# Batch attention: one maximum over 16 batch elements from a single four-bank PSUM buffer, in place of one over 8 from two alternating buffers

## The reference, cut to what matters

```python
scores = jnp.einsum('bqhd,bkhd->hbqk', Q, K)
attn = jax.nn.softmax(scores, axis=1)        # axis 1 is the batch, 32 elements
heads = jnp.einsum('hbqk,bkhd->bqhd', attn, V).reshape(B, S, dm)
```

## Time and profile before

| | us |
|---|---|
| median of 3 runs | 1695.55 |
| lowest and highest run | 1689.3, 1696.78 |
| the profiled execution, its own time | 1693.03 |
| its span in the profile | 1691.3 |
| busy: TensorE matmul, VectorE, GpSimd, ScalarE | 1392.7, 1242.4, 1029.3, 885.9 |

### The profile page before, as it was taken

One profiled execution on the slowest core, in us unless ns is written; L12 is line 12 of the kernel. 1 busy time (PEld: TensorE's weight loads), 2 busy tenths in 40 slices (PEclk: granted clock), 3 DMA queues, 4 the chain that ended last, 5 costly groups with the idle time before them and its releaser, 6 DMA issues. The chain is left out here.

```text
span 1691.3 us, 42035 instructions
## 1 busy us (share of the span) xinstructions
PE 1392.7 (82%) x14758; PEld 1078.4 (64%) x14759; DVE 1242.4 (73%) x2603; ACT 885.9 (52%) x1437; POOL 1029.3 (61%) x746
## 2 busy tenths in 40 slices
PE   7858999999999999998189968888888099999940
PEld 5635666666666666665179966667667099999940
DVE  5559999999999999998356646999998523333346
ACT  7818888888888888887034422222222044444420
POOL 6624888888888888889534432656556544444420
PEclk9859999999999999999589988999999599999975
DMA  6863333333333333310533321222221122222248
GB/s 221 270 197 95 77 83 82 83 82 84 82 82 83 84 80 86 81 50 18 138 123 99 94 60 59 90 94 82 89 93 54 50 63 68 66 65 65 65 138 289
DMA packets 117937, 163.58 MB, mean 97 GB/s; under 512 B 18592, under 2 KB 85408, under 8 KB 113184
## 3 DMA queue, kind: packets, MB, share of 16 engines
q1 hardware_dynamic: 92960, 123.42, 26.3%
q0 software_dynamic: 13600, 28.45, 5.1%
q10 hardware_dynamic: 11232, 9.73, 1.8%
HBM read 99.52 MB, written 62.01 MB: 96 GB/s over the span
## 5 line engine op out<-in xcount | busy, mean ns | idle before, releaser
L921 ACT ACTIVATE Ex<-pB 128x512 f32<-128x512 f32 x512 | 514.3, 1081 | 84.5 <-PE pB L731 80.2
L962 POOL TENSOR_TENSOR V<-Ex,R 128x4096 f32<-128x4096 f32 x64 | 474.2, 7409 | 98.8 <-DVE R L841 98.7
L819 DVE TENSOR_REDUCE mg<-pA 128x128 f32<-128x1024 f32 x256 | 297.5, 1203 | 3.7 <-PE pA L714 3.4
L835 DVE TENSOR_REDUCE Z<-Ex 128x64 f32<-128x2048 f32 x128 | 290.7, 2273 | 4.6 <-ACT Ex L921 4.5
L731 PEld LDWEIGHTS pB<-qk 72*128 72x128 bf16 x2048 | 157.7, 97 | 122.5 <-issue 1.1
L726 PE MATMUL pB<-mh,identb 128*128 128x512 bf16 x512 | 196.6, 384 | 36.0 <-ACT Ex L921 35.4
L1113 POOL DMA_INDIRECT y_d<-x1yb,x1xb x136 | 130.2, 957 | 151.4 <-DVE x1yb L1228 146.8
L731 PE MATMUL pB<-qk 72*128 72x128 bf16 x2048 | 198.9, 219 | 0.0
L726 PE MATMUL pB<-ml,identb 128*128 128x512 bf16 x512 | 194.0, 379 | 0.0
L741 PE MATMUL pO<-V,Vh 128*8 128x128 f32 x4096 | 161.0, 278 | 12.9 <-POOL V L962 12.8
L714 PE MATMUL pA<-qk 72*128 72x128 bf16 x2048 | 162.5, 224 | 8.8 <-DVE mg L819 4.9
(11 more groups left out here) (232 smaller groups left out, 2368.1 us busy)
## 6 DMA issues: line engine op xcount, KB each, us to landing
qk<-qs_d SPq DMA_DIRECT2D x96, 192.0 KB
qk<-ks_d SPq DMA_DIRECT2D x96, 192.0 KB
x1xb<-xs_d SPq DMA_DIRECT2D x136, 64.5 KB
f_ye<-y_d SPq DMA_DIRECT2D x16, 512.0 KB, 5.9
qs_d<-parts SPq DMA_DIRECT2D x16, 384.0 KB, 2.9
ks_d<-parts SPq DMA_DIRECT2D x16, 384.0 KB, 3.2
x0xb<-xs_d SPq DMA_DIRECT2D x72, 64.5 KB
xn_d<-xn SPq DMA_DIRECT2D x16, 258.0 KB, 3.3
```

Source lines behind the costliest of these rows:

```text
L819: dve.tensor_reduce(mg[:, :, g], pA[:, g % 2, :, :].rearrange("p b q -> p q b"), AX.X, ALU.max).then_inc(b_red, 1)
L835: dve.tensor_reduce(Z[:, q], Ex[:, j, q, :], AX.X, ALU.add).then_inc(b_sum, 1)
L921: act.activation(Ex[:, j, :, BG * g:BG * (g + 1)].rearrange("p q b -> p b q"), pB[:, g % 2, :, :], ACT.Exp).then_inc(b_exp, 1)
L962: pool.tensor_tensor(En[:, j % 2, :, :].rearrange("p b q -> p q b"), Ex[:, j, :, :], R[:, j % 2, :].unsqueeze(2).broadcast_to([P, P, B]), ...
```

## The change

A group now has 16 batch elements, and there are two groups to a unit. `pA` has the same four banks, but they are one buffer: every group of first scores waits for the maximum of the group before it. In the loop turn of a unit the first scores stand at `g = 0` and `g = 4` in blocks of 16 matmuls, where blocks of eight stood at 0, 2, 4 and 6. VectorE has one maximum ahead of the first half sum and one behind it, where it had one and three. `mg` shrinks to two columns.

```diff
-            GM = 2 * BG
+            GM = 4 * BG
...
-            pA = pb("pA", [P, 2, GM, P], ph)
+            pA = pb("pA", [P, GM, P], ph)
...
-                    if not isinstance(n, int) or n >= 2:
-                        pe.wait_ge(b_red, n - 1)
+                    if not isinstance(n, int) or n >= 1:
+                        pe.wait_ge(b_red, n)
                     for c in range(GM):
                         tok = (GM * g + c) * P
-                        ins = nc.tensor.matmul(pA[:, g % 2, c, :],
+                        ins = nc.tensor.matmul(pA[:, c, :],
...
                         for g in range(0, NBG, 2):
-                            s1(g // 2)
+                            if g % (NBG // NM) == 0:
+                                s1(g // (NBG // NM))
...
-                    dve.tensor_reduce(mg[:, :, g], pA[:, g % 2, :, :].rearrange("p b q -> p q b"),
+                    dve.tensor_reduce(mg[:, :, g], pA[:].rearrange("p b q -> p q b"),
                                       AX.X, ALU.max).then_inc(b_red, 1)
...
                             group_max(u + 2, 1)
-                            group_max(u + 2, 2)
-                            group_max(u + 2, 3)
                             unit_max(u + 2, (j + 2) % 4)
```

## The result

The changed kernel's median is 1679.94 us over 8 runs (1678.02 to 1685.04). The kernel before, run beside it, has 1689.1 us over 8 runs. The ratio is 0.9943, with a 95% interval of 0.9924 to 0.9961: 9.6 us less, or 0.6%. The three runs from which the forecast had its base (1695.55) are among those eight, and two of them are the highest (1696.78 and 1695.55). So the forecast time of 1680.5 was met more closely than the step was: 15 us were forecast and about 10 came.

What follows compares the result with a forecast made beforehand. VectorE was taken to bound the kernel at 10.56 us a unit, then TensorE and ScalarE's loop at 10.24. With -15.0 the span goes from 1691.3 to 1676.3, execution 1678, plus 2.5 gives 1680.5 us; range 1670 to 1694.

Steps and rivals of the forecast that it cites:

- What bounded the kernel before: Batch-attention stage: VectorE never waits and sets the period of 10.56 us; TensorE's loop behind it takes 9.7.
- VectorE's side: VectorE's work per unit: long maximum 2.23 us, shorter unit maximum 0.42, period 10.10, so 0.46 less.
- U: VectorE's maximum over a unit's group maxima: reads 256 instead of 512 elements, from 0.69 to 0.42 us.
- Rival C: VectorE's long maximum costs more than the slope, 2.35 to 2.43 us: period 10.34 to 10.50, time 1688 to 1698; chance 0.16.
- TensorE's side: Loop of TensorE and ScalarE takes over at 10.24 us per unit; only 0.32 of the 0.46 comes out.
- The added wait: Score blocks wait for maxima with one buffer: covered by 1.1 and 1.8 us; VectorE idles 0.14 per unit.
- Rival D: Score block's wait for the maximum falls on TensorE's path: a unit takes 11.0 us, time 1728; chance 0.08.
- The start: Start of the stage, refill uncovered: first second scores 6.8 us later, unit maximum of unit 3 6.2 later.
- The sum: Whole stage: 58 periods of 10.24 us from unit 3 to unit 61, after the slower start; difference -15.0 us.
- X: Start of a unit's second score block on TensorE; forecast at 165.4 us for unit 3, 759.3 for unit 61.
- Rival E: Granted clock below 1.00 between 140 and 750 us, counted among the slower outcomes; chance 0.02.
- Rival B: VectorE stays the bound and all of 0.46 us per unit comes out: period 10.10, time 1674; chance 0.19.

Runs made afterwards that it cites:

- the copy for the reciprocal: Copy of Z in place of its reciprocal: in the changed kernel 1683.15 us, against 1679.94; in the kernel before 1664.79 us, against 1689.97.
- the split kernel: The changed kernel with each block of 16 first-score matmuls cut into halves of eight around the even second scores: 1673.29 us, ratio to before 0.9907.

## Why the prediction was right, point by point

**What bounded the kernel before.** Right: the copy for the reciprocal brings the period to 10.13 there and does not shorten that of the changed kernel.

**VectorE's side.** U at 0.42: exact. The long maximum lasts 2.23 behind R and 2.29 behind a half sum; the forecast had 2.23 for both, though it used 1.215+1.07 = 2.28 for the start. VectorE's own sum is 10.16, as the split kernel shows, against 10.10. Rival C falls: 1024 further elements cost 1.07 us in either place (1.16 to 2.23, 1.22 to 2.29), so there is no price for the banks, and 0.06 for the place in the order.

**TensorE's side.** Right: the change of bound, by the two experiments that move it. 10.24 was forecast and 10.30 measured, and the whole difference was a term that the row of the kernel before could not show. There, exp 0 never waited for its scores, since it stood in a queue behind exp 7. The term s2 to exp was read at exp 2 (411.62 to 412.48), and taken for exp 0 too. Without the wait in the way it is 10.23.

**The added wait.** Right in the steady state: no stop of TensorE's matmuls on a maximum, cover about 1 us (the maximum of 406.88 ends at 409.11, and its block starts at 410.23). Rival D occurred only while the phases were settling: TensorE waits 0.22 for the maximum at the block of 152.57 and 0.50 at that of 162.73, in the turn of unit 3.

**The start.** Right, 6.2 forecast and 6.2 measured. The first s2 comes 130.02-113.11 = 16.9 us after the first maximum starts, against 126.64-116.65 = 10.0 before: 6.9 later, 6.8 forecast. No run shows the 4.28 us of a round as such, on which the forecast's first s2 rests, nor what decides when the granted clock rises, on which its M1 of unit 2 at 139 and U of unit 3 at 150.7 rest: both were the author's estimates. In their place the changed kernel's trace shows rounds of 4.27, one of them 4.34 (in the first, maximum 2.28, then 0.06 to the block, and 1.93 from the block to the next maximum), and M1 of unit 2 at 135.66, 22.5 us after the first maximum, where 139 less 116.65 is 22.3. The granted clock rose between 129 and 130 before, 12 to 13 us after the first maximum, and at 133 now, 20 us after it:

```profile
131.00:133.00 2.00, 2.00 (x12) 1.10 (x11) 1.55 (x1) 1.23 (x2) 0.00 (x0) 0.50 0.67 145
133.00:134.00 1.00, 0.76 (x7) 0.43 (x6) 0.00 (x0) 1.00 (x2) 0.00 (x0) 0.97 0.64 169
```

**The sum.** It was mis-sized: -15.0 forecast, -10.3 measured within the stage. 3.8 of the 4.7 are 58 periods of 10.305 instead of 10.24 (X of unit 3 at 162.73, of unit 61 at 760.43), 3.5 of it the 0.06 above and the rest the first five periods, which were 10.34 to 10.38. 0.9 is the X of unit 3, which came that much later than 165.4 less the 3.5 by which this execution was ahead. Half of it is the wait of 0.50 just named. The direction, the order of the terms and the place of every one held. That the median came within 0.6 us of the forecast is luck: the base of 1695.55 stood 6.4 above the 1689.1 of all eight runs, and the step was forecast 5.4 too large (15.0 against 9.6 by the medians), and the two errors cancel. The 2.5 us that were added for the median over the profiled execution did not show again either: the profiled execution of the changed kernel took 1680.1, its median is 1679.94.

**The clock.** Rival E, a clock below 1.00 between 140 and 750 us, falls: the granted clock is 1.00 in all windows from 140 to 750 us, with three short stops of TensorE's matmuls in a unit (four of its weight loads).

**The busiest engine.** Rival B would have had the whole saving come out. VectorE is still the busiest by its time, 10.19 of 10.30 us:

```profile
401.04:411.34 10.30, 10.10 (x145) 6.50 (x144) 10.19 (x7) 8.88 (x11) 8.92 (x4) 1.00 0.27 61
```

And yet taking 0.7 us a unit from it did not shorten the period: it was 10.39 us with the copy.

## What to carry to other kernels

When one engine sets the period, write out the next loop behind it before you shorten its work: here 0.40 us a unit came off VectorE, and 0.26 came out. Ask what waits for the work behind a block before you make the block longer: here the blocks of 16 in front of TensorE's queue delayed the exps, with the sum of TensorE's work unchanged; cutting them in two around the first s2 that ScalarE waits for gave the rest back (10.30 to 10.16). The single buffer was no loss where VectorE's other work covered the refill: with the split blocks a maximum starts 2.18 after the half sum ahead of it, as in the kernel before. It was a loss at the start, where VectorE has no other work and waits 1.5 to 2.0 for each of the first blocks, 6.2 us in all, so look at the start of a pipeline by itself.

## What the runs showed that was not expected

A separate, long fulfilled wait in ScalarE's queue costs 0.06 us in front of an instruction that is itself held up, and nothing in front of one that is ready (exp 0 and exp 4, at 0.92 or 0.86 us after their scores, in three kernels). A reduction of 128x2048 from PSUM lasts 2.23 us straight behind the reciprocal and 2.29 behind a half sum; the same held for 128x1024, 1.16 and 1.22. With the copy in place of the reciprocal it lasts 2.29 and 1.22 there too; what makes the difference is not shown. And the first maximum started anywhere from 110.78 to 116.65 us in ten profiled executions with the same work ahead of it. That is more than half of the effect of this change, so a difference of spans is to be taken within the stage.
